# Four graph-attention layers on one core: tiles taken in pairs in one transfer, a new tile order, sums ahead of the next tile's scores, and unnormalized exponents in layer 1

## What is computed

```python
h = relu(layernorm(x)); x = x + gat0(h, adj)    # layer 0: 4 heads, leaky 0.2, then elu
h = relu(layernorm(x)); x = x + gat1(h, adj)    # layer 1: 1 head, leaky 0.01: h @ W + att @ h
h = relu(layernorm(x)); x = x + gat2(adj, h)    # layer 2: 4 heads, leaky 0.2
h = relu(layernorm(x)); x = x + attn3(h, adj)   # layer 3: q.k scores, 4 heads
# gat: e = leaky(s_i + s_j) where adj, else -inf; alpha = softmax(e, axis=j); out = alpha @ Wh
```

## Time and profile before

| | |
|---|---|
| median of 3 runs | 2129.19 us |
| the profiled execution, its own time | 2130.05 us |
| its span (first to last instruction) | 2128.2 us |
| mean granted TensorE clock | 0.548 of full |
| busy: VectorE / GpSimd / ScalarE / TensorE | 1493.0 / 1116.8 / 535.5 / 511.3 us |
| layer 0, from the first gather to the last step's statistics | about 263 to 702 us |
| layer 1 | about 710 to 1136 us |
| layer 2 | about 1145 to 1613 us |
| layer 3 | about 1630 to 2128 us |

### The profile page before, as it was taken

How to read it: one execution, slowest core, us unless ns; L and a number is a source line. 1 busy time by engine, 2 the same in 40 slices (tenths; PEclk the granted TensorE clock), 3 DMA queues, 4 the chain that set the end, 5 groups by cost and what they waited for, 6 DMA issues and landing times.

```text
span 2128.2 us, 11346 instructions
## 1 busy us (share of the span) xinstructions
PE 511.3 (24%) x2092; PEld 263.6 (12%) x2092; DVE 1493.0 (70%) x2390; ACT 535.5 (25%) x2035; POOL 1116.8 (52%) x1201
## 2 busy tenths in 40 slices
PE   5752011122222212323333224344444000000000
PEld 3531000011111101111111101111111000000000
DVE  4789537687879465768876547476574596798777
ACT  3320022233234111112212112223223222233233
POOL 0000676655763476567643755575542576574762
PEclk8665555555555555555555556566666555555555
DMA  9998694433442353344432533354333575575761
GB/s 357 390 391 317 186 209 109 111 96 101 120 116 69 108 126 105 106 111 132 113 91 72 129 105 114 104 143 121 109 103 127 159 226 181 178 216 154 224 199 48
DMA packets 171381, 328.54 MB, mean 154 GB/s; under 512 B 40094, under 2 KB 83111, under 8 KB 171304
## 3 DMA queue, kind: packets, MB, share of 16 engines
q0 software_dynamic: 65920, 197.88, 34.1%
q1 hardware_dynamic: 82600, 104.48, 14.7%
q10 hardware_dynamic: 22784, 25.40, 3.5%
HBM read 288.94 MB, written 38.72 MB: 154 GB/s over the span
## 4 chain that ended last, share of the span: by engine, by line
DVE 44%; issue 21%; another core or an unknown queue 16%; DMA 7%; ACT 6%; PE 4%; POOL 1%; ACTq 1%; SPq 0%; DVEq 0%; POOLq 0%
DVE s_y L1333 14%; DMA s_adj<-in_adj_dram 5%; DVE s_sc L1251 4%; DVE s_ring L1249 4%; DVE s_ring L1317 4%; DVE s_y L1345 3%; DVE ps L1342 2%; PE ps L1475 1%; DVE s_xs L1366 1%; ACT s_pr L902 1%; POOL s_ring L738 1%; DVE s_stat L1002 1%; DMA s_ring<-s_tab,s_idx 1%; DVE s_sc L1236 1%
## 5 line engine op out<-in xcount | busy, mean ns | idle before, releaser
L738 POOL DMA_INDIRECT s_ring<-s_tab,s_idx x1104 | 1049.1, 950 | 749.6 <-issue 362.9
L1333 DVE TENSOR_REDUCE s_y<-s_ring 128x256 f32<-128x2304 f32 (+4 forms) x96 | 429.4, 4473 | 0.1
L1317 DVE TENSOR_TENSOR s_ring<-s_ring,ps 128x2304 f32<-128x2304 f32 (+4 forms) x96 | 260.9, 2718 | 15.5 <-DVE ps L1270 8.9
L902 ACT ACTIVATE s_pr<-s_sc,s_least 128x9 f32<-128x9 f32 (+12 forms) x416 | 124.0, 301 | 322.0 <-issue 169.7
L1262 DVE RECIPROCAL s_total<-s_total 128x4 f32<-128x4 f32 (+1 forms) x128 | 21.8, 170 | 234.6 <-ACT s_pr L902 105.4
L1514 PE MATMUL ps<-s_wx,s_hT 128*128 128x258 f32 (+1 forms) x256 | 134.8, 682 | 141.0 <-issue 78.5
L1506 PE MATMUL ps<-s_wx,s_hT 128*128 128x512 f32 x128 | 113.3, 1038 | 227.3 <-ACT s_hT L867 124.4
L727 POOL DMA_INDIRECT s_pay<-s_pay_t,s_rank_i x32 | 31.4, 980 | 220.5 <-DVE s_rank_i L1112 211.0
L922 ACT ACTIVATE s_ring<-s_ring,s_pr 128x64 f32<-128x64 f32 x384 | 98.9, 335 | 157.7 <-issue 109.9
L1249 DVE TENSOR_TENSOR s_ring<-s_ring,ps 128x2304 f32<-128x2304 f32 (+12 forms) x32 | 86.9, 2715 | 27.8 <-DMA s_ring<-s_tab,s_idx 27.0
L1486 PE MATMUL ps<-s_ident,s_tb 128*128 128x128 f32 x64 | 22.1, 449 | 346.6 <-ACT s_tb L858 147.4
(11 more groups left out here) (169 smaller groups left out, 1145.0 us busy)
## 6 DMA issues: line engine op xcount, KB each, us to landing
s_adj<-in_adj_dram SPq DMA_DIRECT2D x32, 2048.0 KB, 19.8
s_ring<-s_tab,s_idx POOLq DMA_INDIRECT x1104
s_tab<-s_tb ACTq DMA_DIRECT2D x32, 256.0 KB
s_ring<-s_tab SPq DMA_DIRECT2D x32, 256.0 KB
s_ring<-s_pay SPq DMA_DIRECT2D x32, 132.0 KB
s_tab<-s_tb ACTq DMA_DIRECT2D x32, 132.0 KB
s_ring<-s_tab SPq DMA_DIRECT2D x32, 132.0 KB
s_tab<-s_pay_t ACTq DMA_DIRECT2D x16, 260.0 KB, 6.9
```

Source lines behind the costliest of these rows:

```text
L738: e.indirect_dma_start(g[:, k, 0:L.row], None, self.tab_d[L.n], bass.IndirectOffsetOnAxis(ap=self.idx[:, t, k:k + 1], axis=0)).then_inc(se ...
L902: m = e.activation(p[:, :, h], s[:, :, h], ACT.Exp, bias=self.least[:, j, h:h + 1], scale=-1.0, accum_out=self.total[:, j, h:h + 1])
L1317: e.tensor_tensor(g, g, wide(p, 3, L.hd), ALU.mult).then_inc(self.weighed)
L1333: e.tensor_reduce(y, g[:, :, 0:D].rearrange("p k d -> p d k"), AX, ALU.add).then_inc(self.agg)
```

## The change

1. ORDER is another one. The K of the steps are now 5, 3, 6, 6, 7, 7, 7, 5, 6, 6, 12, 5, 9, 4, 23, 7, 14, 8, 10, 10, 13, 8, 11, 8, 12, 8, 11, 8, 10, 9, 9, 9. Steps 2i and 2i + 1 stand side by side in the ring.
2. Own rows of two tiles are loaded in one transfer, and table rows of two tiles are stored in one. The load of a pair waits for what its second tile must wait for; the store of a pair is issued with the second tile.
3. Layers 0 to 2: VectorE sums a tile ahead of the next tile's scores. In layer 0 it comes to `vec_normal` only after finish and statistics. The last tile's scores come after the finish and the statistics of the one before.
4. ScalarE: in layer 0 `act_below(n)` stands ahead of `act_exp(n + 1)`.
5. Layer 1: the exponents go unnormalized into PSUM, ScalarE writes them there itself; VectorE weighs with them at once, and the finish multiplies the sum by the reciprocal (one VectorE instruction fewer a tile).

```diff
-ORDER = (31, 29, 27) + sum(((n, 26 - n) for n in range(12)), ()) + (12, 14, 13, 28, 30)
+ORDER = (29, 31, 23, 25, 20, 21, 19, 28, 24, 26, 3, 27, 12, 30, 0, 22, 1, 18, 7, 9, 2, 15, 6, 16, 4, 17, 5, 14, 8, 10, 11, 13)
...
+        sizes = [(KS[t] + 1) * self.slot + (D if n == 3 else 0) for t in ORDER]
+        for m, size in enumerate(sizes):
+            at = 0 if m % 2 == 0 and at + size + sizes[m + 1] > FLOATS else at
...
     def sp_own(self, e, L, n):
-        if L.after[n]:
-            e.wait_ge(self.agg, T * L.n + L.after[n])
...
+        if L.after[n + 1]:
+            e.wait_ge(self.agg, T * L.n + L.after[n + 1])
+        src = self.pair(self.pay_d if L.n == 0 else self.tab_d[L.n][0:N, :], n)
+        a = D if L.n == 0 else 0
+        own = [L.at[m] + KS[ORDER[m]] * L.slot for m in (n, n + 1)]
+        self.sp_dma(e, self.both(own[0], own[1], L.mine), src[:, :, a:a + L.mine], self.own_sem(n))
+        if L.n == 3:
+            self.sp_dma(e, self.both(own[0] + L.slot, own[1] + L.slot, D), self.pair(self.q_d, n), self.own_sem(n))
...
     def act_row(self, e, l, n):
-        e.wait_ge(self.tabbed, T * l + n + 1)
-        if l < 3:
-            e.dma_start(self.tab_d[l][rows, 0:D + 2 * H], tb[:, 0:D + 2 * H],
...
+        if n % 2:
+            e.wait_ge(self.tabbed, T * l + n + 1)
+            e.dma_start(self.pair(self.tab_d[l][0:N, :], n - 1)[:, :, 0:w], self.tb[:, (n - 1) % 4:(n - 1) % 4 + 2, 0:w],
+                        allow_slow_non_contiguous=True).then_inc(self.tab_sem(n), 16)
+            if l == 3:
+                e.dma_start(self.pair(self.q_d, n - 1), self.tb[:, (n - 1) % 4:(n - 1) % 4 + 2, 2 * D:3 * D],
...
     def act_exp(self, e, L, n):
         e.wait_ge(self.scored, T * L.n + n + 1)
+        if L.n == 1:
+            p = self.weight_bank(L, n)
+            if n > 1:
+                e.wait_ge(self.weighed, T + n - 1)
...
     def act_layer(self, e, L):
-            if n + 1 < T:
-                self.act_exp(e, L, n + 1)
             if l == 1:
                 self.act_below(e, n)
+            if n + 2 < T:
+                self.act_exp(e, L, n + 1)
             self.act_scale(e, l, n)
             self.act_hidden(e, l, n)
+            if n + 2 == T:
+                self.act_exp(e, L, n + 1)
...
     def vec_normal(self, e, L, n):
         e.wait_ge(self.p_ok, T * L.n + n + 1)
+        if L.n == 1:
+            e.reciprocal(self.share[:, j:j + 1], total).then_inc(self.normal)
+            return
...
     def vec_finish(self, e, L, n):
+        elif L.n == 1:
+            e.wait_ge(self.normal, T * L.n + n + 1)
+            e.scalar_tensor_tensor(x, y, self.share[:, n % 2:n % 2 + 1], x, ALU.mult, ALU.add).then_inc(self.x_new)
...
     def vec_layer(self, e, L):
         for n in range(T):
+            last = n + 2 >= T
             self.vec_weigh(e, L, n)
-            if n + 1 < T:
+            if L.n == 3 and not last:
                 self.vec_ahead(e, L, n + 1)
             self.vec_sum(e, L, n)
-            if L.n:
-                self.vec_finish(e, L, n)
-                if l < 4:
-                    self.vec_stats(e, l, n)
+            if L.n < 3 and not last:
+                self.vec_ahead(e, L, n + 1)
+            if L.n == 0 and n > 2:
+                self.vec_apart(e, n - 3)
+            self.vec_finish(e, L, n)
+            if l < 4:
+                self.vec_stats(e, l, n)
+            if n + 2 == T:
+                self.vec_ahead(e, L, n + 1)
             if n + 1 < T:
                 self.vec_normal(e, L, n + 1)
-            if L.n == 0:
-                if n > 2:
-                    self.vec_apart(e, n - 3)
-                self.vec_finish(e, L, n)
-                self.vec_stats(e, l, n)
```

More of the change, by code:

```diff
@@ L545, in landed, with own_sem, both, pair @@
         return 16 * (L.n * every(T) + every(n + 1))
+    def own_sem(self, n):
+        return self.own_in[n // 2 % 4]
     def own_landed(self, L, n):
         return 16 * ((4 * L.n + n // 8 + 1) if L.n < 3 else 12 + 2 * (n // 8 + 1))
+    def both(self, a, b, w):
+        skip = 0 if 2 * b - a <= FLOATS else b - a - w
+        two = self.ring[:, a - skip:2 * b - a - skip].rearrange("p (t w) -> p t w", t=2)
+        return two[:, :, skip:skip + w]
+    def pair(self, table, n):
+        a, b = ORDER[n:n + 2]
+        return table.rearrange("(t p) d -> p t d", p=P)[:, a:b + 1:b - a, :]
+    def tab_sem(self, n):
+        return self.tab_out[n // 2 % 2]
     def units(self, l, n):
@@ L634, in sp_sorted @@
             self.sp_dma(e, self.vals[:, 8 * g:8 * g + 8, :], pay[:, 8 * g:8 * g + 8, 2 * D + 8:PAY], self.vals_in[g])
-        for n in range(LEAD):
+        for n in range(0, LEAD, 2):
             self.sp_own(e, LAYERS[0], n)
-        for g in (7, 6, 0, 5, 1, 4, 2, 3):
+        for g in (7, 5, 6, 4, 0, 3, 1, 2):
             self.sp_dma(e, self.xs[:, 4 * g:4 * g + 4, :], pay[:, 4 * g:4 * g + 4, 0:D], self.xs_in[g])
@@ L644, in sp_own @@
     def sp_own(self, e, L, n):
-        t = ORDER[n]
-        rows, k = slice(P * t, P * t + P), KS[t]
-        g = self.rows(L, n)
-        if L.after[n]:
-            e.wait_ge(self.agg, T * L.n + L.after[n])
-        if L.n == 0:
[L652 to L657, removed]
+        if L.after[n + 1]:
[6 more added lines that the diff above has]
+            self.sp_dma(e, self.both(own[0] + L.slot, own[1] + L.slot, D), self.pair(self.q_d, n), self.own_sem(n))
     def sp_layer(self, e, L):
         if L.n:
-            for j in range(4):
-                e.wait_ge(self.tab_out[j], self.stored(L.n, 28 + j))
+            for j in range(2):
+                e.wait_ge(self.tab_out[j], self.stored(L.n, 30))
             self.sp_own(e, L, 0)
@@ L665, in sp_layer @@
             self.sp_sorted(e)
-        for n in range(LEAD if L.n == 0 else 1, LEAD):
+        for n in range(LEAD if L.n == 0 else 2, LEAD, 2):
             self.sp_own(e, L, n)
@@ L673, in sp_layer @@
             self.sp_dma(e, self.sym_d, self.sym_i(), self.sym)
-        for n in range(LEAD, T):
+        for n in range(LEAD, T, 2):
             if L.n == 1 and n == T - 4:
@@ L869, in act_row @@
     def act_row(self, e, l, n):
[L871 to L874, removed]
+        H = LAYERS[l].heads
+        tb, o, w = self.tb[:, n % 4, :], self.bank(self.project_bank(l, n)), D + 2 * H if l < 3 else 2 * D
         e.wait_ge(self.projected, T * l + n + 1)
         if l > 1:
-            e.wait_ge(self.tab_out[n % 4], self.stored(l, n - 4) if n >= 4 else self.stored(l - 1, 28 + n))
+            e.wait_ge(self.tab_sem(n), self.stored(l, n - 4) if n >= 4 else self.stored(l - 1, 28 + n))
         if l == 1:
@@ L1275, in vec_ranks @@
         k = KS[t]
[L1276 to L1277 removed]
+        e.tensor_copy(self.idx[:, t, 0:k], self.rows(LAYERS[0], n)[:, 0:k, D + 4])
     def vec_mutual(self, e, n):
@@ L1310, in vec_weigh @@
         p = self.weight_bank(L, n)
-        e.wait_ge(self.normal, T * L.n + n + 1)
+        if L.n == 1:
+            e.wait_ge(self.p_ok, T * L.n + n + 1)
+        else:
+            e.wait_ge(self.normal, T * L.n + n + 1)
         if L.n == 3:
@@ L1584, in _ @@
                 with e.Else():
-                    for j in range(4):
-                        e.wait_ge(s.tab_out[j], s.stored(3, 28 + j))
+                    for j in range(2):
+                        e.wait_ge(s.tab_out[j], s.stored(3, 30))
                     e.nop().then_inc(halt)
```

29 lines of the change are left out of this document (11 added, 18 removed).

## The result

The changed kernel takes 2121.85 us (median of 20 runs) against 2129.92 us for the kernel before: a ratio of 0.9952, 95% interval 0.9934 to 0.9971. Measured twice more it gave 0.9969 (0.9934 to 1.0003) and 0.9929 (0.9900 to 0.9958). The kernel before, timed a second time as if it were a new one, gave 0.9967 (0.9936 to 0.9998) against itself. By the medians the gain is 8, 4 and 12 us, hardly more than the 0.33% by which the kernel before differed from itself; 58 had been forecast.

A forecast was written before the change was run, and what follows sets the result against it. The prediction took the waits between VectorE and the gather stream, neither engine itself, as the bound. Its terms, -91.3 + 10 + 20 + 6 + 10 - 4 - 6.6 - 2.5 = -58, gave 2071 us, range 2005 to 2145.

The forecast's parts named there:

- the order's term: Moving the 23 gathers from step 3 to step 14 removes 91.3 us of VectorE's gather waits; 10 and 20 come back.
- 297 us in all: Idle time of layers 0 to 2 without gather waits, 85, 82 and 130 us, put down to late signals of unknown cause.
- 5 us a layer: Gather waits returning at the big tiles, K = 12 and K = 23: +20 us in all, bounds 0 and 88.
- The sign that the prediction had set for a wrongly costed order: A VectorE wait of 10 to 16 us ahead of the scores of the K = 23 tile.
- The sum first: VectorE's sum ahead of scores: exponents lose cover, +6 us in layer 2, +10 in layer 0 (up to +38), 0 in layer 1.
- The plain exponents: Layer 1, one VectorE instruction fewer in each of 32 tiles: -6.6 us, bound -29.
- Pairs: Paired loads and stores of two tiles: 0, since loads are early and ScalarE is idle beside the stores.
- layer 0's order of finish: Scores and cast cover `act_below` in layer 0, shortening waits at L1362: -4 us, bound -17.5.
- end of layer 2: The 18.1 us from layer 2's last statistics to the next gather shorten by 2.5 us, the last store being double.
- B: Rival, chance 0.14: the wait only moves, to K = 12 and K = 23, and cover is missed; about 2120 to 2140 us.
- A: Rival, chance 0.20: late signals grow as GpSimd gathers with fewer breaks, +93 us, 2164 us; decides from 58 us of growth.
- C: Rival, chance 0.10: late signals all but vanish and layers 0 to 2 come down to the gathers' time; about 1895 us.

The follow-up runs named there:

- the repeat: The kernel before with the new order of tiles alone, run and profiled once more: ratio 1.0013 to the kernel before.
- the quiet set: A set of runs of kernel variants in which the kernel before took 1842.5 us, every other set 2111 to 2159, and hardly any signal was late in profiles.
- the shorter lead: The changed kernel with GpSimd running only to the third tile from the one being summed, not the fourth, in layers 0 to 2: ratio 0.9788, again 0.9758.
- the first set: The set of runs that timed parts of the change alone against the kernel before, which took 2132.46 us there.
- `rest`: The changed kernel with a GpSimd pause of about 2.3 us ahead of every second tile in layers 0 to 2: ratio 1.0255 to the kernel before.

## Why the prediction was wrong

**The step that failed is the order's term: "The 91.3 us go", with 10 and 20 coming back.** Alone the order measured nothing twice (0.9985, 1.0013), in place of 61 us. The premise that failed with it is that the waits for late signals, "297 us in all", stay as they are when another wait goes. Three things are in it.

First, 27.0 of the 91.3 was misread. The row has no step, and I gave it to step 3. The timeline of the kernel before shows what waited:

```profile
1639.80 1.22 DVE L1249 TENSOR_TENSOR s_ring<-s_ring,ps 128x1024 f32<-128x1024 f32 x1 [26.99 <-DMA s_ring<-s_tab,s_idx]
```

1024 numbers are 4 rows of 256, the tile of K = 3 at step 0: the start of the layer, which no order removes. At step 3 layer 3 waited 0.7 us. The term was 65.0. The 10 us for five gathers at step 0 were too many: VectorE's waits at steps 0 to 2, counted from the layer's first gather, went from 38.1 to 39.5 us.

Second, more came back at K = 23 than 5 us a layer: 13.6 + 0 + 14.9 + 12.9 = 41.4 us. The argument was that each late signal lets GpSimd run ahead; the waits say it had run ahead far enough in layer 1 alone, and in the repeat not there either (13.1 + 4.8 + 14.4 + 12.3 = 44.6). That leaves 24 us of gain.

Third, and this took what was left in layers 0 to 2: late waits there rose by 40 us (260 to 300, and 259 to 303 in the repeat), more than the 32 us (27 in the repeat) by which gather waits fell. The sum had taken them as fixed. Half of the sums left out shows that they are not: 206 us of work less, 186 us of late waits more, and 28 more ahead of layer 0's finish. In layer 3 late waits fell by 22 us in this trace, but 16 us more went by between its last gather and the end (40.5 to 56.8; 45.7 in the repeat), where four tiles of K = 10 and 9 now stand. Why signals are late, and so why the waits grow when others go, stays open. The sign that the prediction had set for a wrongly costed order is in the changed kernel's rows: waits of 11.4 and 12.5 us ahead of the scores of the K = 23 tile.

**The sum first.** The terms, +6 in layer 2 and +10 in layer 0, came out at 3.9 and 14 us. I had excluded layer 1, which paid 11, and layer 2's late waits fell by 15, so the agreement is in part luck. Missing altogether was that VectorE's instructions overlap less in the new order: 12.1 us more of busy time, twice, in layers 0 to 2. The sign "VectorE's busy time falls by 6 us in layer 1 alone" failed by it. In total the part cost 0.4 and 1.0%.

**The plain exponents.** -6.6 forecast, 6.7 us of VectorE's time measured: the right size. The kernel's time did not show it (1.0008), which the interval, 0.9975 to 1.0042, would not have told from a gain of 0.3%.

**Pairs, layer 0's order of finish, end of layer 2.** For the pairs 8 us by the medians, not clear of noise, where 0 had been taken. The waits ahead of `vec_finish` in layer 0 were 18.3 us before and 19.7, 16.3 and 18.0 in the changed kernel's three profiles, in place of 4 less. From VectorE's last instruction of layer 2 to layer 3's first gather it took 17.7 us before and 14.0 after, 3.6 less for the 2.5 forecast; the order alone does it too (13.2, and 13.8 in the repeat), so it is not the paired store that does it.

**The rivals.** The time is B's (2120 to 2140), by B's waits in half and by A's growth in the rest. A's late signals did grow, by 28, 53 and 65 us in three profiles; the last is past the 58 us at which A was to decide, and the time stayed below that of the kernel before, with 62 us less of gather waits in that profile. The coincidence that spoke for A, waits that end just after GpSimd's last gather before a break, is no rule. Of ScalarE's eight waits of over 12 us at L881 and L884 in layers 1 and 2 of the kernel before, five end in a break of GpSimd of over 1 us, and three do not, as this one:

```profile
1237.78 0.95 POOL L738 DMA_INDIRECT s_ring<-s_tab,s_idx  x1 [0.30 <-issue]
1238.00 0.38 ACT L884 ACTIVATE s_tb<-ps 128x256 f32<-128x256 f32 x1 [15.50 <-issue]
```

In all sixteen profiles with late signals it is 37 of 100 such waits, while breaks fill about a quarter of the time.

C, the late signals gone, is nothing that the change does; the quiet set shows it of other kernels, and the kernel before took 1842.5 us there.

One slip besides, which moved no term: "Every layer is 80 to 120 us longer" than 345 us does not hold for layer 3, which is 150 us longer.

**What the change is worth without late signals** was not measured. The nearest: in the quiet set, with the wait for landed gathers in both, the changed kernel (with the shorter lead as well) took 1927.44 us and the kernel before 1964.41, 37 less. Layer 3, which carries no added wait, was 430.0 to 430.5 us long with the new order and 433.1 with the old: 22.3 us of waiting at step 3 went, 15.1 came at steps 14 and 16, and the end after the last gather grew from 32.9 to 41.1.

## What to carry to other kernels

A wait that is taken out is worth something only if the next thing that is late is not waiting behind it: before summing gains, leave out a large piece of the suspected engine's work and see whether the time follows (here 206 us of work gave 14). Give each long wait its step by the shape of the instruction that waited, not by the row of its group. Where idle time is of unknown origin, profile one kernel twice and in another set before counting on any of it: late waits in layer 2 of one and the same changed kernel were 104, 138 and 133 us.

## What the runs showed of the hardware

Signals between instructions, even of an engine to itself, came up to 24 us late in layers in which gathers were being issued (ScalarE to itself by 8.83 us five times in one profile of the changed kernel, VectorE to itself by 1.2), and in another set of runs, on variants of the same kernels, next to never (2.5 to 6.1 us of late waits in three layers). The kernel before took 2132 us in the first set and 1842.5 in the quiet one, 14% less; that late signals are the whole of this difference was not profiled. Mean durations of VectorE's weighing and summing (2.71 and 4.48 us) and GpSimd's period of 1.25 us were the same in both, and so was the time from the start of the last gather before a break of over 4 us to the end of its last packet (median 2.8 us in the kernel before, 2.9 in `rest`); what differed is when a signal was seen.

Loading of instructions is not what makes signals late. The pages of the kernel before and of `rest`, late and quiet, count alike:

```profile
q14 instruction: 58, 0.48, 0.1%
```

```profile
q14 instruction: 58, 0.47, 0.1%
```

and in the trace of the kernel before no such packet starts between 1454.6 and 1531.2 us, while ScalarE waited from 1492.5 to 1515.8.

Holding GpSimd back came with fewer late waits: waiting for landed gathers at every second tile took late waits from 288 to 179 us, one tile less of lead to 229 and 242, and both gave 2%; a pause of 0.94 us at every tile took nothing (284). In the quiet set the same wait cost 6% on the kernel before. Whether the landing or the length of the break counts stays open: the two kernels made to tell it fell into the quiet set. What differs between the sets stays open too; the record gives chip 0 for the first set and for the quiet one alike. For the same reason no version is named the best: the shorter lead (2086 us; 0.9788 and 0.9758) and the wait for landed gathers (2087 us; 0.9783) are the fastest with late signals, and without them the two together cost 4.5%.

The Trainium skill ("VectorE: DVE Perf Modes", "The TRN2 errata — SBUF-src ops pay a fixed extra latency per instruction") warns that completion increments of semaphores at a high rate from one engine can deadlock another. Nothing deadlocked here, and no run shows whether the lateness has to do with it.
